# Cross-attention and a mixture of experts in one kernel: the seam between the last heads and the first expert tiles

## The chip, the cores and the metric

One program on one NeuronCore of a Trainium2 chip. The metric is the time of one execution on the device in microseconds (us), here the median of a few runs. The engines are TensorE (PE in the rows, its weight load PEld), VectorE (DVE), ScalarE (ACT), GpSimd (POOL) and SyncE (SP, which only issues transfers).

## The reference, cut to what matters

Sizes: 32 batches of 112 tokens, width 256; 8 heads of 64; 375 context rows beside 112 latents; 8 experts of width 1024, two of them chosen for each token.

```python
x = x + tanh(g_xattn) * xattn(ctx, layernorm(x), mask, ...)      # 8 heads, softmax, @ Wout
h = layernorm(x)
bids = sigmoid(h @ conf_w.T + conf_b) * wealth
top_bids, selected = top_k(bids, 2)
routing = softmax(top_bids)                                      # weights of the two experts
ffn(e) = (silu(h @ gate_w[e].T) * (h @ up_w[e].T)) @ down_w[e].T
x = x + tanh(g_ffn) * sum over the two experts of routing * ffn(e)
```

## The kernel before, in words

All products run on TensorE as three f16 products of a split high and low half (`PARTS`), so most tiles have a "hi" step on ScalarE and a "lo" step on VectorE.

**Attention.** A function `body(b, ...)` on each engine (571 on GpSimd, 766 on ScalarE, 1210 on VectorE, 1550 on TensorE) is written out for batches 0 to 31 and two more turns, 32 and 33, in which only what is left of the last batches runs. A batch has eight slots h, one for each head. In a slot VectorE masks the scores and takes their minimum (`masked_max`, L986), ScalarE takes the exponential (L732), TensorE transposes (L1493), ScalarE and VectorE split the result (`probs_hi` L739, `probs_lo` L992) and TensorE multiplies with the values (oP). The last two heads of a batch are finished in slots 0 to 2 of the next turn. One batch's heads are joined and projected in the next turn too (`heads_out`, `heads_T`, `out_proj`, `residual`), then `rstd1` on GpSimd, `norm2`, `norm2_T`, and one turn later `confidences` and `logits`.

**Routing.** Batches are routed in quads of four. `route` (1049) has 20 steps, small VectorE operations that each wait for the one before: `choose` (0 to 13), `route_rank` (14), `weigh_choice` (15, 16), `place` (17 to 19). `ranks` (1532) counts on TensorE between steps 13 and 14. Then GpSimd scatters the quad's token rows to `routed_rows` in DRAM (`scatter`, L557), two indirect transfers for each batch. The last quad, batches 28 to 31, is routed in two pairs by the table `PAIR_AT`; its rows go out by `scatter_pair`. `QUAD_AT` and `LAST_QUAD_AT` place the steps of the other quads.

**Experts.** Eight experts follow as 63 tiles of 128 routed rows each, in the order of their counts (`order_experts`). `step(t, ...)` runs a tile: `gate_up` (1625) in two halves i of 512 columns, `silu` (L874), `gated` (L1352), `down` (1650) for the tile before, `weigh` (L1365), and an adding scatter into `out` (`add_tile`, L622). The tile's rows come by `load_tile` (564). The first `AHEAD` = 4 tiles have known addresses (`first_i`) and are loaded in turn 32; later ones read theirs from `tile_table` (1396), 18 small VectorE operations which end in `s_tab`. There are `XT_BUFS` = 6 buffers. An expert's weights come as six pieces (`raw`), are squared (`expert_squares`, L826), scaled (`expert_bound`, `expert_pow` L520, `expert_scale`) and split (`expert_hi` L836, `expert_lo` L1204).

**Order.** It is written by hand: each engine executes its own list in order, and semaphores hold an instruction until another engine has counted far enough. Nothing is moved by a scheduler. SyncE's list matters as well: `turn_of` (373) issues a batch's loads and stores, `load_raw` (385) the first two experts' pieces, and between them stand the eight writes of zero rows (`padrows`, L421) behind each expert's rows. In turn 31 of GpSimd's list `rstd1` stands behind four scatters:

```python
                if b == B - 1:
                    scatter(q - 1, 0)
                    scatter(q - 1, 1)
                ...
                if holds(b, 1, B):
                    rstd1(b - 1)
                if b == B - 1:
                    expert_pow(0)
```

## Time and profile before

| what | value |
| --- | --- |
| time, median of 3 runs | 1455.01 us (1454.85 to 1457.35) |
| the profiled execution | 1453.81 us |
| its span, first to last instruction | 1452.2 us |
| busy: PE, PEld, DVE, ACT, POOL | 94%, 67%, 70%, 64%, 33% |
| mean granted TensorE clock | 0.986 of full speed |
| chain that ended last | PE 33%, DMA 3%, all else 1% or less each |
| instructions | 41651 |

The page cuts the span into 40 slices of 36.3 us. TensorE's row reads 9 in nearly all of them, and lower in the first, in slices 23 to 26 and in the last: start, the seam between attention and experts, and end. "Waits" and "idle before" are time in which an engine had nothing to run, with what released it; matmul ends are modelled, so a busy TensorE is not one at its peak.

### The profile page before, as it was taken

The numbers are of one execution on the slowest core, as the hardware profiler recorded it, in microseconds if no ns is written. First come the engines' busy times: TensorE is split into PE (matmuls) and PEld (weight loads), VectorE is DVE, ScalarE is ACT, GpSimd is POOL, SyncE is SP. The second block draws the span as 40 slices with busy tenths as digits, with TensorE's granted clock in tenths as the row PEclk, the third lists the DMA queues.
The fourth block names the chain that finished last, engine by engine and source line by source line (L and its number), as shares of the span: only waits on it lengthen the run. The fifth ranks groups of instructions, "written<-read, shape, count | busy, mean of one in ns | idle before, by whom it ended". The sixth has DMA issues, their size and how long they took to land. (4 is left out here: it accounts for less than half of the span.)

```text
span 1452.2 us, 41651 instructions
## 1 busy us (share of the span) xinstructions
PE 1359.2 (94%) x13880; PEld 972.9 (67%) x13880; DVE 1019.2 (70%) x2553; ACT 933.3 (64%) x1940; POOL 485.9 (33%) x655
## 2 busy tenths in 40 slices
PE   2999999999999999999999958999999999999996
PEld 1466666666666666666666646777877778877784
DVE  4788888888888888888888875665546654334442
ACT  5687877787887878777777765556656553333331
POOL 4323233333433333333432143333344332222221
PEclk9999999999999999999999968999999999999998
DMA  4010101111111101111110335433366743112461
GB/s 117 26 41 26 42 26 43 34 41 46 39 48 32 54 29 41 45 33 53 35 37 14 114 109 157 106 82 94 103 206 175 229 153 91 31 31 34 117 201 16
DMA packets 54866, 107.16 MB, mean 74 GB/s; under 512 B 10832, under 2 KB 32720, under 8 KB 54672
## 3 DMA queue, kind: packets, MB, share of 16 engines
q0 software_dynamic: 23712, 55.71, 14.9%
q1 hardware_dynamic: 30112, 47.75, 10.5%
q8 instruction: 127, 2.08, 0.6%
q10 hardware_dynamic: 848, 1.07, 0.3%
q14 instruction: 67, 0.55, 0.1%
HBM read 69.16 MB, written 35.34 MB: 72 GB/s over the span
## 5 line engine op out<-in xcount | busy, mean ns | idle before, releaser
L874 ACT ACTIVATE sg<-gP,consts 128x512 f32<-128x512 f32 x126 | 86.4, 686 | 240.3 <-PE uP L1435 240.3
L1352 DVE SCALAR_TENSOR_TENSOR act_h<-uP,consts,sg 128x512 f32<-128x512 f32 x126 | 94.6, 750 | 206.8 <-ACT sg L874 202.8
L1435 PE MATMUL fP<-zTs,ws 128*128 128x112 f16 (+1 forms) x1536 | 220.5, 294 | 11.4 <-DVE zT L963 5.6
L1435 PE MATMUL fP<-ws,zTs 128*128 128x512 f16 x768 | 186.8, 379 | 0.5 <-DVE kT L976 0.2
L986 DVE CUSTOM_DVE_ANT_0 ms<-simP,madd,sim_undo 112x488 f32<-112x488 f32 x256 | 183.9, 719 | 3.4 <-remote 0.9
L732 ACT ACTIVATE pr<-ms,nmax 112x488 f32<-112x488 f32 x256 | 179.0, 699 | 4.3 <-DVE nmax L986 1.2
L1435 PEld LDWEIGHTS fP<-zTs,ws 128*128 128x128 f16 x1536 | 109.9, 99 | 102.9 <-issue 34.4
L992 DVE SCALAR_TENSOR_TENSOR pT<-ptP,pT 122x448 f16<-122x448 f32 x256 | 157.5, 615 | 30.3 <-ACT pT L739 29.5
L1435 PE MATMUL yP<-W,aT 128*128 (+1 forms) x1512 | 175.4, 273 | 2.5 <-DVE aT L1358 2.5
L1435 PEld LDWEIGHTS yP<-W,aT 128*128 128x128 f16 x1512 | 147.6, 98 | 33.5 <-issue 3.9
L739 ACT ACTIVATE pT<-ptP 122x448 f16<-122x448 f32 x256 | 137.8, 538 | 42.3 <-PE ptP L1493 39.1
L622 POOL DMA_INDIRECT out<-ysb,xt x63 | 105.3, 1672 | 170.9 <-DVE ysb L1365 162.3
L1435 PE MATMUL oP<-v,pT 122*128 122x64 f16 x3072 | 133.5, 194 | 12.4 <-DVE pT L992 7.4
L1493 PE MATMUL ptP<-ident,pr 112*122 112x112 f32 x1024 | 142.3, 261 | 0.5 <-DVE filled L1097 0.5
L1435 PEld LDWEIGHTS oP<-v,pT 122*128 122x128 f16 x3072 | 120.9, 98 | 24.8 <-DVE pT L992 24.6
L497 POOL TENSOR_TENSOR zTs<-zT,zTs 128x1200 f16<-128x1200 f32 x31 | 76.5, 2469 | 174.3 <-ACT zTs L713 174.3
L1493 PEld LDWEIGHTS ptP<-ident,pr 112*122 112x122 f32 x1024 | 115.0, 140 | 25.2 <-issue 1.2
L1435 PEld LDWEIGHTS fP<-ws,zTs 128*128 128x128 f16 x768 | 68.0, 98 | 82.1 <-issue 14.4
L1483 PE MATMUL simP<-kT,qT 64*128 64x488 f16 x768 | 101.5, 368 | 14.5 <-DVE nmax L986 12.3
L976 DVE SCALAR_TENSOR_TENSOR kT<-fP,kT 128x488 f16<-128x488 f32 x128 | 84.8, 663 | 36.6 <-ACT kT L725 36.6
L725 ACT ACTIVATE kT<-fP 128x488 f16<-128x488 f32 x128 | 73.9, 577 | 52.0 <-PE fP L1435 51.9
L569 POOL DMA_DIRECT2D xt<-routed_rows x63 | 36.0, 574 | 211.0 <-issue 181.3
(220 smaller groups left out, 2557.2 us busy)
## 6 DMA issues: line engine op xcount, KB each, us to landing
raw<-wffn POOLq DMA_DIRECT2D x36, 512.0 KB, 6.3
split_experts<-W POOLq DMA_DIRECT2D x12, 1024.0 KB
W<-split_experts SPq DMA_DIRECT2D x16, 768.0 KB
xc<-ctxt SPq DMA_DIRECT2D x32, 375.0 KB
xt<-routed_rows POOLq DMA_DIRECT2D x63, 129.0 KB, 2.5
raw<-wffn SPq DMA_DIRECT2D x12, 512.0 KB, 8.2
xl<-x SPq DMA_DIRECT2D x32, 112.0 KB
xres<-x SPq DMA_DIRECT2D x32, 112.0 KB, 4.5
```

The lines of the kernel that those rows point to most:

```text
L497: nc.gpsimd.tensor_tensor(zTs[p][:, 1, :, :], zT[:, :, :], zTs[p][:, 0, :, :], ALU.subtract).then_inc(s_zsplit, 1)
L622: pool.indirect_dma_start(out[:, :], bass.IndirectOffsetOnAxis(ap=xt[k][:, D:D + 1].bitcast(I32), axis=0), ysb[t % 2][:, :], None, compute ...
L732: nc.scalar.activation(pr[h % 2][:, :], ms[h % 2][:, :], ACT.Exp, bias=nmax[p][:, h:h + 1], scale=-1.0, accum_out=rsum[p][:, h:h + 1]).the ...
L739: nc.scalar.activation(pT[h % 2][:, 0, :, 0:S], ptP[h % 2][0:KR, :, 0:S], ACT.Copy, scale=P_TOP).then_inc(s_pthi, 1)
L874: nc.scalar.activation(sg[i][:, :], gP[i][:, :], ACT.Silu, scale=constant(place, 0)).then_inc(s_silu, 1)
L976: nc.vector.scalar_tensor_tensor(out=o, in0=i, scalar=1.0 / TOP, in1=hi, op0=ALU.mult, op1=ALU.subtract).then_inc(s_plo, 1)
L986: nc.vector.tensor_tensor_reduce(out=ms[h % 2][:, :], in0=simP[h % 2][0:S, 0:NK], in1=madd[p][:, :], scale=sim_undo[0:S, 0:1], scalar=3.0e ...
L992: nc.vector.scalar_tensor_tensor(out=pT[h % 2][:, 1, :, 0:S], in0=ptP[h % 2][0:KR, :, 0:S], scalar=P_TOP, in1=pT[h % 2][:, 0, :, 0:S], op0 ...
L1352: nc.vector.scalar_tensor_tensor(out=act_h[i][:, :], in0=uP[i][:, :], scalar=constant(place, 2), in1=sg[i][:, :], op0=ALU.mult, op1=ALU.mu ...
L1435: last = nc.tensor.matmul(o, lhs(k, a), rhs(k, c), start=n == 0, stop=n == len(todo) - 1)
L1483: last = nc.tensor.matmul(simP[i][:, 0:NK], qT[p][r, a, h // 2, :], kT[p][r, c, h // 2, :], start=t == 0, stop=t == len(PARTS) - 1)
L1493: last = nc.tensor.transpose(ptP[h % 2][0:KR, c, 0:S], pr[h % 2][:, c * KR:(c + 1) * KR], ident[0:S, 0:S])
```

## The change

The added turns 32 and 33 are gone. After batch 31 each engine has a list `tail()` written out by hand, in which the rest of batch 31 and tile 0 stand side by side, and the tile loop starts at t = 1. In `step` t = 1 to 3 stand the remaining parts of the last batch.

- TensorE: the products of tile 0 (`gate_up(0, ...)`) follow the last head's values; `heads_T(31)`, `out_proj(31)`, `norm2_T(31)` and `confidences(31)` stand between products of tiles 0 and 1, `ranks` of the last quad in step 2.
- Expert 0: its pieces are loaded before turn 32's transfers, squared in batches 29 and 30 (`SPLIT_SQ`) instead of 31, scaled in slots 2 and 3 of batch 31, split in slots 5 to 7 and the tail (`SPLIT_AT`).
- Routing: the last quad is routed as one, in steps 1 and 2 (`close`); its scatters go in GpSimd's steps 2 and 3 (`scatter_last`). The weights of the two experts come from a tanh instead of an exponential and a reciprocal. The copies of its token rows move from ScalarE to GpSimd (`copy_last`).
- The tile table is cut into `tile_counts` (step 2), `tile_places` and `tile_rows` (step 3). `AHEAD` is 5, so tile 5 is the first that is loaded by the table; that load stands in GpSimd's step 3 behind the last scatters. Zero rows behind each expert grow from 3 to 5 tiles (`PADT`).
- Expert 1: squares one to a tile (`SQUARES_1`), scale after `tile_rows` at the end of step 3, split in steps 4 and 5.

```diff
-PADT = -(-(2 * S + P - 1) // P)
+PADT = -(-(4 * S + P - 1) // P)
-AHEAD = 4
+AHEAD = 5
+SQUARES_1 = {0: (0,), 1: (1,), 2: (2, 3, 4), 3: (5,)}
+HI_1 = {4: (0, 1, 2), 0: (3, 4, 5)}
-SPLIT_SQ = {(B - 1, h): (h,) for h in range(PIECES)}
-SPLIT_AT = {(B - 1, 7): (0, 1), (B, 0): (2,), (B, 1): (3,), (B, 2): (4,), (B, 6): (5,)}
+SPLIT_SQ = {(B - 3, 7): (0,), (B - 2, 1): (1,), (B - 2, 2): (2,), (B - 2, 5): (3,), (B - 2, 6): (4,), (B - 2, 7): (5,)}
+SPLIT_AT = {(B - 1, 5): (0,), (B - 1, 6): (1,), (B - 1, 7): (2,)}
...
@@ GpSimd @@
+            def tail():
+
+                pool.wait_ge(s_pv, (B - 1) * H + 6)
+                scatter(QUADS - 2, 2)
+                pool.wait_ge(s_ao, B)
+                scatter(QUADS - 2, 3)
+                copy_last(B - 4)
+                copy_last(B - 3)
+                copy_last(B - 2)
+                rstd1(B - 1)
+                copy_last(B - 1)
...
             def step(t, k):
+                if t == 2:
+                    scatter_last(0)
+                    scatter_last(1)
+                if t == 3:
+                    scatter_last(2)
+                    scatter_last(3)
+                    for i in range(4):
+                        pool.wait_ge(s_scat[i], 32 * QUADS)
+                    pool.wait_ge(s_tab, 1)
+                    for n in range(AHEAD, XT_BUFS):
+                        load_tile(n, n)
...
+                if t == 3:
+                    load_tile(6, 6 % XT_BUFS)
+                if 3 <= t < NT - 4:
                     load_tile(t + 4, (t + 4) % XT_BUFS)
                 p = t // SPAN + 1
                 if p < E and t % SPAN == 3:
                     expert_pow(p)
@@ ScalarE @@
+            def tail():
+
+                probs_hi(B - 1, H - 2)
+                expert_hi(0, 3)
+                tile_hi(0, 0)
+                probs_hi(B - 1, H - 1)
+                norm2_out(B - 2)
+                expert_hi(0, 4)
+                silu(0, 0, 0)
+                heads_out_hi(B - 1)
+                tile_hi(1, 1)
+                act_hi(0, 0, 0)
+                expert_hi(0, 5)
+                silu(0, 1, 0)
+                for c in SQUARES_1[0]:
+                    expert_squares(1, c)
@@ VectorE @@
+                if t == 3:
+                    tile_rows()
+                    expert_scale(p)
...
+            def tail():
+
+                probs_lo(B - 1, H - 2)
+                expert_lo(0, 3)
+                tile_lo(0, 0)
+                probs_lo(B - 1, H - 1)
+                sums_inverse(B - 1, 1)
+                heads_out(B - 1, 1)
+                logits(B - 2, (B - 2) % 4)
+                expert_lo(0, 4)
+                gated(0, 0, 0)
+                heads_out_lo(B - 1)
+                tile_lo(1, 1)
+                act_lo(0, 0, 0)
+                expert_lo(0, 5)
+                gated(0, 1, 0)
+                residual(B - 1, 1)
```

TensorE's list, from the last transposition of batch 31 to the second half of tile 0. oP is the last head's product, tP batch 31's joined heads, projection, second norm and confidences, ptP the ranks, xP and gP, uP tile 0. Before:

```order
L1435 MATMUL oP<-v,pT 128x64 [waits s_ptlo]
L1435 MATMUL oP<-v,pT 128x64 x11
L1537 MATMUL ptP<-both,earlier_h 112x2x8 [waits s_ptlo,s_oh]
L1511 MATMUL tP<-ident,ao 128x112 [waits s_z2c,s_ao]
L1435 MATMUL tP<-ws,aoT 112x256 [waits s_aolo]
L1522 MATMUL tP<-ident,z_3 128x112 [waits s_z2]
L1529 MATMUL tP<-confT,z2T 112x8 [waits s_lg,s_z2c]
L1612 MATMUL xP<-ident,xt 128x128 [waits s_xt0]
L1435 MATMUL gP<-xT,W 128x128 [waits s_xtlo,s_there,s_wlo]
```

Now:

```order
L1712 MATMUL xP<-ident,xt 128x128 [waits s_xt0]
L1610 MATMUL tP<-ident,z_2 128x112 [waits s_z2]
L1523 MATMUL oP<-v,pT 128x64 [waits s_ptlo]
L1617 MATMUL tP<-confT,z2T 112x8 [waits s_lg,s_z2c]
L1523 MATMUL gP<-xT,W 128x128 [waits s_xtlo,s_wlo]
L1599 MATMUL tP<-ident,ao 128x112 [waits s_z2c,s_ao,s_lg]
L1712 MATMUL xP<-ident,xt 128x128 [waits s_xtlo,s_xt1]
L1523 MATMUL tP<-ws,aoT 112x256 [waits s_aolo]
L1523 MATMUL gP<-xT,W 128x128 [waits s_xtlo,s_act,s_there,s_wlo]
L1610 MATMUL tP<-ident,z_3 128x112 [waits s_z2]
```

Five waits of batch 31 stood ahead of tile 0's first product; four of them now stand behind it, and the ranks further back still.

GpSimd's list in its steps 2 and 3, behind the first adding scatter (the stores to routed_rows are the last quad's). Now:

```order
L569 DMA routed_rows<-zrow,slot_i 30336x258 [waits s_padw,s_slots,s_zcopy]
L636 DMA out<-ysb,xt 3712x256 [waits s_add,s_yw]
L579 TENSOR_LOAD t_row_i [waits s_scat3,s_scat2,s_tab,s_scat1,s_scat0]
L581 DMA xt<-routed_rows 128x258
L579 TENSOR_LOAD t_row_i [waits s_add]
L521 TENSOR_TENSOR epow<-ebound,minus_half 128x3 [waits s_ech]
L636 DMA out<-ysb,xt 3712x256 [waits s_yw]
```

Four pairs of stores stand around the second row, two on each side; three loads of tiles (5, 6 and 7) stand between the third row and the power of expert 1.

VectorE's list at the end of step 3. The first t_row is the table's, ebits and the ones behind it are the scale of expert 1, act_h is the first half of tile 4. Now:

```order
L1402 TENSOR_SCALAR ysb<-yP,xt,consts 128x256 [waits s_add,s_down,s_ech]
L1502 TENSOR_REDUCE t_row<-past_jump 1x64 [waits s_tabch]
L1508 TENSOR_SCALAR t_row_i<-t_row 1x64 [waits s_tabch]
L1238 TENSOR_SCALAR ebits<-epow 128x3 [waits s_epow]
L1245 RECIPROCAL consts<-eundo 128x2 [waits s_ech]
L1389 SCALAR_TENSOR_TENSOR act_h<-uP,consts,sg 128x512 [waits s_atlo,s_silu,s_ech]
L1395 TENSOR_TENSOR aT<-aP,aT 128x512 [waits s_athi]
```

Before, the whole table stood ahead of tile 0's first act_h; now its last part stands between tiles 3 and 4, with the scale of expert 1 behind it.

## Rows read from the trace of the kernel before

**Rows 1.** Stretches: length, busy PE, PEld, DVE, ACT, POOL, PEclk, DMA share, GB/s.

```profile
780.00:830.00 50.00, 47.78 (x489) 30.93 (x486) 40.13 (x105) 34.98 (x80) 9.21 (x10) 1.00 0.24 83
845.00:882.00 37.00, 19.07 (x150) 16.13 (x151) 27.85 (x99) 15.72 (x33) 17.52 (x21) 0.54 0.62 189
900.00:1440.00 540.00, 535.94 (x5458) 425.83 (x5455) 275.09 (x467) 252.64 (x420) 170.28 (x173) 1.00 0.42 112
```

**Rows 2.** Chain that ended last, in the seam and tile 2: start, us, what.

```profile
857.65 0.53 DVE pT L992
...
859.58 0.69 DVE ao L1004
...
862.78 2.82 PE tP L1435 x12
...
877.08 2.72 PE gP L1435 x24
...
893.32 1.34 PE gP L1435 x24
...
896.44 0.22 PE xP L1612 x2
...
901.87 1.34 PE gP L1435 x24
```

**Rows 3.** VectorE in order: heads 0 and 7 of batch 31, table, tile 3.

```profile
829.98 0.72 DVE L986 CUSTOM_DVE_ANT_0 ms<-simP,madd,sim_undo 112x488 f32<-112x488 f32 x1
...
849.32 0.73 DVE L986 CUSTOM_DVE_ANT_0 ms<-simP,madd,sim_undo 112x488 f32<-112x488 f32 x1 [0.22 <-DVE ebound L1187]
...
853.37 2.48 DVE L1204 SCALAR_TENSOR_TENSOR W<-raw,escale,W 128x1024 f16<-128x1024 f32 x2 [0.48 <-ACT W L836]
...
868.17 0.41 DVE L1031 TENSOR_SCALAR z<-x,mv,rs 112x256 f32<-112x256 f32 x1 [1.24 <-POOL rs L514]
...
878.78 0.68 DVE L1407 TENSOR_TENSOR past<-turn,tile_end 1x512 f32<-1x512 f32 x1
...
880.80 0.68 DVE L1414 TENSOR_TENSOR past_jump<-past,jump 1x512 f32<-1x512 f32 x1
...
882.78 0.18 DVE L1418 TENSOR_SCALAR t_row_i<-t_row 1x64 int32<-1x64 f32 x1
...
908.76 0.75 DVE L1352 SCALAR_TENSOR_TENSOR act_h<-uP,consts,sg 128x512 f32<-128x512 f32 x1 [0.55 <-ACT sg L874]
```

**Rows 4.** ScalarE in order: a square in batch 31, expert 0's first splits, the table load.

```profile
831.43 1.04 ACT L826 ACTIVATE junk<-raw 128x1024 bf16<-128x1024 f32 x1
...
852.11 2.19 ACT L836 ACTIVATE W<-raw,escale 128x1024 f16<-128x1024 f32 x2 [0.98 <-DVE escale L1193]
...
875.90 1.28 ACT L874 ACT_TABLE_LOAD   x1
```

**Rows 5.** GpSimd in order: last scatter, tile loads, power of expert 1.

```profile
883.06 0.94 POOL L557 DMA_INDIRECT routed_rows<-zrow,slot_i  x1 [0.30 <-issue]
889.69 0.60 POOL L569 DMA_DIRECT2D xt<-routed_rows  x1 [5.70 <-issue]
890.86 0.56 POOL L569 DMA_DIRECT2D xt<-routed_rows  x1 [0.57 <-issue]
...
909.19 0.92 POOL L520 TENSOR_TENSOR epow<-ebound,minus_half 128x3 f32<-128x3 f32 x1
```

**Rows 6.** The page's part 6, tile loads: KB each, us from issue to landing.

```profile
xt<-routed_rows POOLq DMA_DIRECT2D x63, 129.0 KB, 2.5
```

**Rows 7.** The clock in stretches of 2 us, columns as in rows 1.

```profile
846.00:848.00 2.00, 0.56 (x3) 0.56 (x4) 1.32 (x7) 1.06 (x3) 0.75 (x2) 0.81 0.19 58
...
880.00:882.00 2.00, 2.00 (x25) 2.00 (x23) 1.83 (x6) 0.01 (x1) 1.39 (x3) 0.66 1.05 425
```

**Rows 8.** SyncE's issues in the seam: zero rows, then expert 1's pieces.

```profile
862.70 9.28 SPq L421 DMA_DIRECT2D routed_rows<-padrows  x8
873.05 3.86 SPq L390 DMA_DIRECT2D raw<-wffn  x6
```

More of the change, by code:

```diff
@@ L401, in _ @@
                     turn_of(g * 2 + k, k)
-            for b in range(B, B + 2):
-                turn_of(b, b % 2)
             sp.wait_ge(s_order, 1)
@@ L406, in _ @@
             load_raw(0)
-            for b in range(B + 2, B + 4):
+            for b in range(B, B + 4):
                 turn_of(b, b % 2)
@@ L572, in body @@
                 p = g % 2
-                quad = g == 3 and holds(b, 7, B - 1)
                 if holds(b, 0, B - 2):
@@ L577, in body @@
                     rows_lo(b + 2, p)
+                if g == 0 and holds(b, 8, B - 1):
+                    scatter(q - 2, 0)
                 if holds(b, 0, B - 4):
@@ L613, in _ @@
             pad_outside()
-            for b in range(B + 2):
+            for b in range(B):
                 body(b, b % 4, b // 4)
+            tail()
             def add_tile(t, k):
@@ L1391, in step, with close, tile_counts @@
                     weigh(t - 1, (k - 1) % 4, last_place)
-                if 1 <= done < E and j in LO_LATE:
-                    for c in LO_LATE[j]:
-                        expert_lo(done, c)
-            def tile_table():
+                if t == 3:
+                    tile_rows()
+                    expert_scale(p)
+                if 1 <= done < E and j in late:
+                    for c in late[j]:
+                        expert_lo(done, c)
+            def close(first, end):
+                for step in range(first, end):
+                    route(QUADS - 1, slice(0, 4), step)
+            def tail():
[14 more added lines that the diff above has]
+                residual(B - 1, 1)
+            def tile_counts():
                 count_rows()
@@ L1418, in tile_table @@
                 nc.vector.tensor_scalar(t_row_i[:, :], t_row[:, :], float(E * CAP), None, ALU.min).then_inc(s_tab, 1)
[L1420 to L1425 removed]
+            for b in range(B):
+                body(b, b % 4, b // 4)
+            tail()
+            held_now = 0
+            for t in range(1, NT + 1):
+                last_held, held_now = held_now, None if t == NT else place_of(t)
+                step(t, t % 4, held_now, last_held)
         @block.tensor
@@ L1602, in _ @@
                     piece(0, 0, n)
-            for b in range(B + 2):
-                body(b, b % 4, b // 4)
             def tile_T(t, k):
```

277 lines of the change are left out of this document (151 added, 126 removed).

## The prediction

> **What bounds the kernel now.** I read the stretches first. In the attention stage TensorE is busy 47.8 of 50 us, in the expert stage 535.9 of 540 [rows 1]: both belong to TensorE, and work that other engines do there is covered. In the seam between them TensorE is busy 19.1 of 37 us at a granted clock of 0.54 of full speed, half of it in the lower of its two levels, 1.2 instead of 2.4 GHz. So the seam is where something can be gained, and only by starting the tiles' products earlier, since behind them TensorE has no gap to give.
>
> The chain of waits says what stands in the seam. The low half of the last head ends at 858.2 (857.65 + 0.53), the heads are joined at 859.58, the projection takes 2.82 us, and after the norm and 20 small routing steps the first product of tile 0 starts at 877.08; tile 2 starts at 893.32 and tile 3 at 901.87, so an undisturbed tile costs 8.6 us [rows 2]. I call the start of tile t's products S(t). The effect on the end of the kernel is the shift of S(5), because from there on both lists are the same.
>
> **The sum**, against the profiled execution of 1453.81 us (span 1452.2; 1.2 us below the median of 1455.01, to which I add the same difference).
>
> *First product of tile 0.* Before, 18.9 us pass from the last low half to that product. Now only the last head's values and two small confidence products stand there. Joining starts 1.4 us after the low half [rows 2], which holds the values; the confidences fit in the rest, so I take 1.4. Gain 17.5 us. For this four pieces of expert 0 must be split and tile 0 transposed by then; both stand ahead of the last low half in the new lists, so they belong to the next term.
>
> *The slots of batch 31.* Six squares of 1.04 us leave ScalarE's list there [rows 4], 6.2 us. Into slots 3, 5, 6 and 7 of VectorE come the scale (seven small steps) and splits of 1.24 us, half of 2.48 [rows 3], each behind ScalarE's half of 1.1 [rows 4]. The same four splits stood ahead of the last low half before, so none is new; but the scale, moved up to slot 3, lengthens it on VectorE. Bounds: nothing gained, or all 6.2 us. Head 0 to head 7 took 19.3 us before [rows 3], and I find VectorE's own work, with the waits for ScalarE's splits, to fill most of that. I take 1.0 us, near the lower end.
>
> *From S(0) to S(2).* It was 16.2 us, with the slow clock at its start in both cases. Added on TensorE are the projection, 1.4 us at full clock (half of 2.82 [rows 2]), the transposition of the heads, and two or three products as small as a tile's transposition, 0.22 each [rows 2]: together 2.3. Then one wait: from the end of the projection (865.60) to the second norm's z took 2.6 us and z itself 0.41 [rows 2, 3], 3.0 in all, and now the first half of tile 1 covers 2.7 of it (893.32 to 896.44, less 0.44 of transposition). VectorE has also a gated half-tile to do first; I take 0.8 us of wait. Loss 3.1 us, bounds 2.5 and 5.
>
> *Squares in batches 29 and 30.* ScalarE was busy 35.0 of 50 us there, TensorE 47.8 [rows 1]. Six squares of 1.04 put some 6 us more into a list which TensorE waits for at every piece. Bounds 0 (they fall into its gaps) and 4; I take 1.5 us lost, since the gaps are mostly shorter than a square.
>
> *Ranks in step 2.* Eight tiny products, 0.3 us lost. The pieces of routing in steps 1 and 2 lie on VectorE, half idle there (275 of 540 us [rows 1]): nothing.
>
> *Tile 5.* This is the new wait. TensorE transposes tile 5 at S(4) + 3.1 (893.32 to 896.44 [rows 2]). Its load needs the table's end. In step 3 VectorE does the second gated half at S(3) + 6.9 (908.76 against 901.87 [rows 2, 3]), 0.75 long; then `tile_places`, 2.0 us (878.78 to 880.80); bound and weighing, 1.0; `tile_rows`, 2.2 us (880.80 to 882.96 [rows 3]). That is S(3) + 12.8, or S(4) + 4.2. GpSimd then reads a register, 0.57 [rows 5], and the load lands 2.5 us after its issue [rows 6]: S(4) + 7.3, so TensorE waits 4.2 us. Behind that load GpSimd issues two more, 1.17 us apart (889.69 to 890.86), before the power of expert 1, 0.92 [rows 5]; VectorE's scale waits for it and blocks tile 4's first gated half: 4.2 + 3.5 + 0.9, scale 1.3, gated 0.75, low half 0.6 is S(4) + 11.3, where `down(3)` could have started at 10.1. Another 1.2 us. The clock adds to it: in the stretch in which TensorE did 0.56 us of work in 2 it fell to 0.81 and then to half, and it came back only 3.8 us after dense products began [rows 2, 7]. 3.8 us at half speed lose 1.9, of which the wait for `down(3)` hides 1.2. Loss 4.2 + 1.2 + 0.7 = 6.1 us. Bounds: 3.5 if VectorE is ahead of this (`tile_rows` can't start before step 3's last product), 9.6 if the last scatters land late. They leave GpSimd at S(4) + 2.0 (eight at 1.24 apart, 0.94 + 0.30); behind the last one before, the next load was 5.7 us late [rows 5], though with the transfer engines full.
>
> Sum: -17.5 - 1.0 + 3.1 + 1.5 + 0.3 + 6.1 = **-7.5 us**: 1446.3 for an execution like the profiled one, 1447.5 as a median.
>
> Costed at nothing: two more table loads on ScalarE, 1.28 us each [rows 4], in step 1. They delay tile 1's second silu by about 1.1 us, which the 5.2 us of `down(0)` and the first half of tile 2 cover. The Trainium skill, "ScalarE: Activation LUTs", section "What ACT_TABLE_LOAD costs", gives a switch as about 2.66 us, because the engine also drains. No row here shows the drain. By that page the routing's last choice would come late enough for `ranks` to hold TensorE for an estimated 1.5 us, and the sum would be -6.0.
>
> The earlier zero rows cost nothing either, if only transfers wait for them. They are 5 tiles each instead of 3, so what took SyncE 9.3 us to issue takes up to 15.5, and expert 1's pieces follow [rows 8]. They start some 16 us earlier, as soon as batch 30 is through, and expert 1's first square can hold ScalarE for a microsecond or two which its slack covers.
>
> **Rivals.**
>
> *The squares set the pace of batch 31* (chance 0.24). ScalarE's squares stretched every slot, and without them 5 us are gained instead of 1. For it: each is longer than most of ScalarE's gaps. Against it: VectorE takes on the scale. The sum becomes -11.5, 1443.5.
>
> *Gained at S(0), lost in the tail* (0.14). ScalarE and VectorE serve heads, weights and tiles from one list, and one late entry holds all of them. If the last head comes 3 us later, the norm's wait is 3 us instead of 0.8, and squares cost 3, the sum is -7.5 + 4 + 2.2 + 1.5, about 0: 1455.
>
> *GpSimd makes it slower* (0.10). The second norm's `rstd1` now stands behind two pairs of scatters and three copies, each of which waits for a landed scatter; all that goes on while zero rows and expert 1's pieces fill the transfer engines (share 0.62 of the whole seam before [rows 1]). GpSimd would be ready at about 866, and the norm wants it at about 871. The point from which it decides is a landing more than 5 us later than that. If scatters land only behind the zero rows and the pieces, some 12 us later, TensorE waits 7 us at the second norm, the clock adds 1.9, and the late landing at tile 5 another 3.5: -7.5 + 12.4 = +4.9, 1460. For it: the 5.7 us of [rows 5]. Against it: those are 5.7, not 12. The Trainium skill, "DMA: Bandwidth & Descriptors", section "SWDGE vs HWDGE vs iDMA", says that GpSimd's and SyncE's transfers enter different queues of a DMA engine, which takes them in turn; by that a scatter isn't kept behind all zero rows, and this rival goes. No run here shows it yet.
>
> **How the numbers follow.** The forecast has 0.52 and is the likeliest. A measurement of this kernel tells about 0.2%, 2.9 us, from no change. Forecast and first rival are faster (0.76), the second the same (0.14), the third slower (0.10). The terms' bounds taken together give -17.4 and +1.4; the range for 8 in 10 reaches from halfway to the best ends, 1441, to the second rival's 1455.5.
>
> **What would show it.** Right: tile 0's first product within 2 us of the last head's values, and 19 us before the old place; a wait of TensorE for tile 5's rows in step 4 of about 4 us, with GpSimd's load just behind the table's last step; `ebits` waiting for `epow` behind it; the clock low again for about 4 us. Wrong: no wait at tile 5, or one that the scatters end; the second norm's transposition waiting over 2 us; head 7 of batch 31 before 845 or after 851 on its own clock.

## The result, and the profile after

The changed kernel takes 1458.07 us (median of 20 runs, 1454.85 to 1462.77) against 1454.93 for the kernel before (20 runs, 1453.03 to 1457.35): ratio 1.0023, 95% interval 1.0016 to 1.0031. It is slower by 0.23%, where 0.5% faster was forecast. The profiled execution took 1456.04 us, its span 1454.1, at a mean clock of 0.987; span and clock of before were 1452.2 and 0.986.

A call is one sitting on one chip, in which kernels are timed side by side. The calls fall into two kinds, in which the kernel before takes 1453 to 1455 us or 1444 to 1446 us (one chip showed both), and each comparison of times is made within one call. I call them the 1455 calls and the 1445 calls; the profiles of this section and of the one ahead of the prediction are of the first kind.

TensorE in order in the changed kernel: the first products of tiles 0, 2, 3, 4 and 5, i.e. S(0) and S(2) to S(5), with what is between.

```profile
856.86 2.72 PE L1523 MATMUL gP<-xT,W 128*128 128x128 f16 x24
...
870.60 0.41 PE L1610 MATMUL tP<-ident,z 112*128 112x112 f32 x2 [1.01 <-DVE z L1068]
...
877.67 1.50 PE L1523 MATMUL gP<-xT,W 128*128 128x128 f16 x24
...
886.64 1.50 PE L1523 MATMUL gP<-xT,W 128*128 128x128 f16 x24
...
890.42 0.22 PE L1523 MATMUL uP<-xT,W 128*128 128x128 f16 x1 [1.00 <-issue]
890.48 0.29 PE L1747 MATMUL aP<-ident,act_h 128*128 128x128 f32 x1
891.13 0.27 PE L1747 MATMUL aP<-ident,act_h 128*128 128x128 f32 x1 [0.37 <-issue]
...
902.37 0.59 PE L1636 MATMUL bP<-esq,ones 128*128 128x6 f32 x2 [4.89 <-ACT junk L837]
902.82 4.55 PE L1523 MATMUL yP<-W,aT 128*128 128x256 f16 x24
907.21 1.50 PE L1523 MATMUL gP<-xT,W 128*128 128x128 f16 x24
...
913.81 0.69 PE L1712 MATMUL xP<-ident,xt 128*128 128x128 f32 x2 [3.32 <-DMA xt<-routed_rows]
...
920.92 1.50 PE L1523 MATMUL gP<-xT,W 128*128 128x128 f16 x24
```

The first products of tiles 2 to 5 in the kernel before, read in the same way (the chain of [rows 2] has these times 0.16 later):

```profile
893.15 1.50 PE L1435 MATMUL gP<-xT,W 128*128 128x128 f16 x24
...
901.71 1.50 PE L1435 MATMUL gP<-xT,W 128*128 128x128 f16 x24
...
910.40 1.50 PE L1435 MATMUL gP<-xT,W 128*128 128x128 f16 x24
...
918.95 1.50 PE L1435 MATMUL gP<-xT,W 128*128 128x128 f16 x24
```

Tile 0 starts 20.2 us earlier (856.86 for 877.08) and tile 3 still 15.1 (886.64 for 901.71). Tile 4 starts at 907.21, where 910.40 was the time before: 11.9 us are gone inside one tile, which takes 20.6 us instead of 8.7. Tile 5's wait adds 5.2, and S(5) is 920.92 against 918.95: 2.0 us late, as the span is 1.9 longer.

Where the 11.9 us went: ScalarE, then the first and the last of GpSimd's eight stores, then the stretches (columns as in [rows 1]), all of the changed kernel.

```profile
888.24 0.19 ACT L837 ACTIVATION_READ_ACCUMULATOR junk<-raw 128x1 f32 x1
899.14 0.69 ACT L882 ACTIVATE sg<-gP,consts 128x512 f32<-128x512 f32 x1 [10.72 <-remote]
```

```profile
886.11 0.99 POOL L569 DMA_INDIRECT routed_rows<-zrow,slot_i  x1 [3.89 <-DVE slot_i L1175]
...
896.75 0.93 POOL L569 DMA_INDIRECT routed_rows<-zrow,slot_i  x1 [0.30 <-issue]
```

```profile
100.00:780.00 680.00, 661.70 (x6909) 438.32 (x6908) 591.48 (x1634) 541.43 (x1226) 243.14 (x368) 1.00 0.13 39
780.00:830.00 50.00, 47.74 (x492) 30.70 (x491) 39.41 (x101) 38.59 (x89) 9.21 (x10) 1.00 0.27 91
845.00:882.00 37.00, 29.99 (x303) 24.92 (x304) 22.54 (x49) 21.38 (x36) 14.28 (x16) 0.77 0.84 258
884.00:888.00 4.00, 4.00 (x50) 3.71 (x49) 3.58 (x20) 3.60 (x6) 1.59 (x2) 1.00 0.09 25
889.00:899.00 10.00, 6.04 (x27) 2.41 (x24) 0.00 (x0) 0.00 (x0) 6.86 (x7) 0.83 0.38 92
899.00:907.00 8.00, 4.63 (x25) 3.51 (x26) 5.11 (x12) 3.69 (x7) 0.00 (x0) 0.57 0.00 0
```

From 889 to 899 ScalarE and VectorE do nothing at all, and TensorE 27 products, some of them one by one with 0.2 to 1.0 us of "issue" ahead. ScalarE waits 10.72 us for silu(0) of tile 3. Its input was there: the last product of that half is the one at 890.42. The releaser is "remote", i.e. the profile finds none. That product was itself late by 1.0 us, so of the 10.7 us some 2 are a wait for input and 8.5 are not. TensorE's first gap begins 3.3 us behind the first store (889.4 against 886.11), and ScalarE goes on 2.4 us behind the start of the last (899.14 against 896.75). GpSimd alone goes on all the time. The wait of bP for expert 1's last square and the half-clock `down(2)` (4.55 us, clock 0.57) are its wake: that square stands on ScalarE behind the silu.

The lines for tile 5 on VectorE and on GpSimd, SyncE's issues, and the first square of expert 1 and a table load on ScalarE, all of the changed kernel:

```profile
909.87 0.18 DVE L1505 TENSOR_SCALAR t_row_i<-t_row 1x64 int32<-1x64 f32 x1
915.66 0.17 DVE L1238 TENSOR_SCALAR ebits<-epow 128x3 int32<-128x3 int32 x1 [5.61 <-POOL epow L521]
```

```profile
911.42 0.60 POOL L581 DMA_DIRECT2D xt<-routed_rows  x1 [13.73 <-issue]
```

```profile
844.23 13.05 SPq L422 DMA_DIRECT2D routed_rows<-padrows  x8
858.69 8.49 SPq L393 DMA_DIRECT2D raw<-wffn  x6
```

```profile
870.02 1.06 ACT L837 ACTIVATE junk<-raw 128x1024 bf16<-128x1024 f32 x1 [3.91 <-DMA raw<-wffn]
...
874.58 0.23 ACT L779 ACTIVATE ex<-lg 112x32 f32<-112x32 f32 x1
874.83 1.28 ACT L882 ACT_TABLE_LOAD   x1
876.12 0.69 ACT L882 ACTIVATE sg<-gP,consts 128x512 f32<-128x512 f32 x1
```

### The profile page after: what moved, and what is told of

Read it like the earlier page. It is cut to its first block, busy times and chain, and to the rows that moved or that the text cites. A ratio compares the mean times of both kernels' runs of the same rounds, so it can differ in the third digit from the quotient of the medians.

```text
span 1454.1 us, 41488 instructions
## 1 busy us (share of the span) xinstructions
PE 1362.5 (94%) x13880; PEld 972.1 (67%) x13880; DVE 1015.2 (70%) x2528; ACT 931.2 (64%) x1932; POOL 487.5 (34%) x659
## 3 DMA queue, kind: packets, MB, share of 16 engines
q0 software_dynamic: 23712, 55.71, 15.1%
q10 hardware_dynamic: 848, 1.07, 0.3%
## 4 chain that ended last, share of the span: by engine, by line
PE 70%; DVE 9%; ACT 6%; issue 6%; DMA 5%; SPq 1%; POOL 1%; another core or an unknown queue 1%; POOLq 0%; DVEq 0%; ACTq 0%
PE fP L1523 19%; PE yP L1523 10%; PE uP L1523 10%; PE gP L1523 9%; PE simP L1571 5%; PE ptP L1581 4%; PE tP L1523 3%; PE oP L1523 3%; DVE ms L1023 2%; DVE pT L1029 2%; DMA out<-ysb,xt 2%; DMA raw<-wffn 2%; PE aP L1747 2%; DVE ao L1041 1%; ACT z L715 1%
## 5 line engine op out<-in xcount | busy, mean ns | idle before, releaser
L1523 PE MATMUL oP<-v,pT 122*128 122x64 f16 x3072 | 133.5, 194 | 17.4 <-DVE pT L1029 12.6
L1523 PE MATMUL uP<-xT,W 128*128 128x128 f16 x1512 | 106.1, 220 | 1.0 <-issue 1.0
```

The source lines that it names most:

```text
L1523: last = nc.tensor.matmul(o, lhs(k, a), rhs(k, c), start=n == 0, stop=n == len(todo) - 1)
```

## The experiments

S(t) and the span are from one profiled execution of each kernel, in us; the ratio to the kernel before is from all the executions of both in the same call, and not from the medians alone:

| kernel | call | S(0) | S(2) | S(3) | S(4) | S(5) | span | ratio (95%) |
| --- | --- | --- | --- | --- | --- | --- | --- | --- |
| before, first profile | 1455 | 877.08 | 893.15 | 901.71 | 910.40 | 918.95 | 1452.2 | |
| before, e9 | 1455 | 878.25 | 894.80 | 903.35 | 912.04 | 920.59 | 1452.6 | |
| before, e15 | 1445 | 872.32 | 889.21 | 897.76 | 906.45 | 915.00 | 1444.0 | |
| changed, first profile | 1455 | 856.86 | 877.67 | 886.64 | 907.21 | 920.92 | 1454.1 | 1.0023 (1.0016 to 1.0031) |
| changed, e1 | 1455 | 857.38 | 883.45 | 892.42 | 912.49 | 926.20 | 1460.7 | 1.0045 (1.0032 to 1.0058) |
| changed, e10 | 1455 | 857.40 | 880.74 | 889.71 | 910.91 | 924.84 | 1458.0 | 1.0027 (1.0014 to 1.0040) |
| changed, e14 | 1445 | 857.00 | 884.51 | 893.48 | 902.46 | 918.94 | 1453.0 | 1.0024 (1.0014 to 1.0033) |
| no last stores, e2 | 1455 | 857.84 | 882.48 | 891.45 | 900.42 | 914.71 | 1446.7 | 0.9963 (0.9952 to 0.9974) |
| spaced, e3 | 1455 | 857.48 | 884.20 | 893.17 | 902.14 | 919.19 | 1450.9 | 0.9985 (0.9976 to 0.9995) |
| squares later, e11 | 1455 | 856.96 | 876.09 | 885.06 | 905.25 | 920.33 | 1451.7 | 1.0007 (0.9997 to 1.0016) |
| squares later, e7 | 1445 | 856.87 | 876.29 | 885.26 | 894.23 | 910.86 | 1442.0 | 0.9977 (0.9968 to 0.9987) |
| spaced, pieces first, e8 | 1445 | 856.74 | 875.59 | 884.56 | 893.53 | 910.12 | 1438.5 | 0.9972 (0.9962 to 0.9983) |
| the same, e16 | 1445 | 856.84 | 876.65 | 885.62 | 894.59 | 911.61 | 1441.9 | 0.9975 (0.9966 to 0.9984) |
| tile 5 later, e12 | 1455 | 857.33 | 876.97 | 885.94 | 906.44 | 916.29 | 1450.7 | 0.9991 (0.9981 to 1.0002) |
| all together, e13 | 1445 | 856.49 | 876.68 | 885.65 | 894.62 | 908.69 | 1440.1 | 0.9966 (0.9952 to 0.9979) |
| e13, power first, e17 | 1445 | 856.90 | 876.79 | 885.76 | 894.73 | 905.82 | 1435.3 | 0.9959 (0.9946 to 0.9971) |
| the same, e18 | 1455 | 857.06 | 877.28 | 886.25 | 895.22 | 908.92 | 1442.3 | 0.9942 (0.9925 to 0.9958) |

Behind S(5) the lists are the same, but the profiles of this table still need 528.4 to 534.5 us from there to the end. So the span of one execution says less about an edit than the ratio does.

**Is the stall the kernel's, and is it the stores?** e1 is the changed kernel again.

> The changed kernel once more, nothing edited. In its first profile ScalarE's silu of tile 3 stood 10.7 us (888.4 to 899.1) with its inputs there, TensorE went product by product with gaps and VectorE stood too, and S(4) came 20.6 us behind S(3) where 8.7 is normal: 11.9 us lost. If that stall belongs to the kernel, it is there again at the same silu, 8 to 13 us long, and the time is 1458 again. If it is a chance of the one execution, the profile has no idle time of ScalarE over 3 us in tile 3, S(4) is about 895, and the profiled time is about 1444, or the runs spread between 1444 and 1460.

It is there again (silu(0) of tile 3, 9.30 us, S(4) - S(3) = 20.1), 1461.98 us. A second loss shows: ScalarE's first square of expert 1 waited 6.77 us and TensorE 3.19 us for the confidences of batch 31.

```diff
             def step(t, k):
-                if t == 2:
-                    scatter_last(0)
...
-                        pool.wait_ge(s_scat[i], 32 * QUADS)
                 if t == 3:
                     pool.wait_ge(s_tab, 1)
```

> The eight stores of the last quad's rows on GpSimd (four pairs, in tiles 2 and 3) are left out, so the last quad's tokens get no expert output. Theory A: the unbroken series of eight indirect stores on GpSimd, 886 to 898, holds up the other engines. Then the stall is gone, S(4) - S(3) is about 8.8 us instead of 20.6, the wait for tile 5's rows stays (3 to 4 us), and the time is 11 to 13 us less, about 1446. Rival B: the stall sits at a place in ScalarE's or TensorE's instruction list and has nothing to do with the stores: it stays, and the time is 1457 to 1458. Rival C: it belongs to expert 1's squares or the routing's tanh in the same tiles: also unchanged.

1448.33 us, 13.6 less than e1 in the same call. S(4) - S(3) is 8.97, and no wait without a releaser is left. B and C fall: the lists of TensorE, ScalarE and VectorE are unchanged. What went with the stores is GpSimd's wait for their landing.

```diff
                 if t == 2:
                     scatter_last(0)
-                    scatter_last(1)
                 if t == 3:
+                    pool.wait_ge(s_gu, 7)
+                    scatter_last(1)
+                    pool.wait_ge(s_gu, 8)
                     scatter_last(2)
+                    pool.wait_ge(s_act, 8)
                     scatter_last(3)
```

> The same eight stores, but no longer in one row: the first pair in tile 2, the second behind the first half of tile 3, the third behind its second half, the fourth behind its second gated half. Theory A (a long unbroken series is what stalls): the stall shrinks to under 2 us, S(4) - S(3) about 9 to 10.5 us, time 1446 to 1448. Theory A' (each store costs the other engines its share, whatever the spacing): about 10 us are still lost, in four pieces of 2 to 3 us, time about 1457. Rival B: unchanged, one stall of 10 us at the silu of tile 3.

1452.73 us, 9.3 less than e1, and S(4) - S(3) is 8.97. The spacing was poor (a gap of 1.0 us behind the first pair and of 0.3 behind an adding scatter, then six stores in a row), and yet the long stall is gone. What is left of it is short: VectorE waits 1.7 us at 896.8 and again at 905.0, and from the start of the sixth store of the row, 904.02, TensorE's products go one by one (2.37 us of work from 903 to 907), now in step 4:

```profile
903.48 0.50 PE L1526 MATMUL uP<-xT,W 128*128 128x128 f16 x6
904.21 0.22 PE L1526 MATMUL uP<-xT,W 128*128 128x128 f16 x1 [0.23 <-issue]
904.95 0.33 PE L1526 MATMUL uP<-xT,W 128*128 128x128 f16 x3 [0.52 <-issue]
```

So neither "each store costs its share" (10 us) nor a plain count of stores in a row fits. In order, GpSimd had four stores, the adding scatter and four stores without a gap; now it has two, the gap of 1.0 us, the adding scatter and six. Whether the gap or the earlier adding scatter avoids the long stall was not told apart.

```diff
+            for _ in range(100):
+                apart(act)
             for b in range(B):
```

(and the same for TensorE)

> 100 semaphore increments that nobody waits for are put ahead of batch 0 in ScalarE's and in TensorE's list, so that every later instruction lies 100 places further on in the instruction store; the order of the work and the stores are as in the changed kernel. They cost up to about 3 us at the start. Theory A: the stall stays at the silu of tile 3, 8 to 13 us, time 1458 to 1461. Rival B (a fetch of instructions that falls due just there): the stall is gone or sits at another instruction, and the time is 1446 to 1450.

The stall stays at the same silu, 10.69 us, S(4) - S(3) = 20.4: B falls. The time was 1476.98, because the increments, priced at 3 us, cost 14.6 (S(0) 871.98), some 0.15 us each. TensorE stands 14.06 us ahead of its product at 62.06, in batch 0.

**Does any row of eight do it?** e5 is the kernel before with its stores bunched, e6 the changed kernel with plain stores. Both fell into a 1445 call.

```diff
-                if quad and b < B - 1:
-                    scatter(q - 1, 0)
-                if g < 3 and holds(b, 8, B - 1):
-                    scatter(q - 2, g + 1)
+                if g == 0 and holds(b, 8, B - 1):
+                    for i in range(4):
+                        scatter(q - 2, i)
```

> The kernel before, with one edit in the attention stage: the four pairs of indirect stores of each quad 0 to 5, which GpSimd issues one pair a batch some 24 us apart, are issued as one row of eight in batches 8, 12, ... 28. Its trace had no idle time without a releaser there. Theory A (a long unbroken series of indirect stores on GpSimd holds up the other engines): six stalls of TensorE, ScalarE or VectorE appear, each 2 to 10 us long and each beginning 2 to 4 us behind the first store of a series; the time is 12 to 60 us more. If the stall belongs to the seam alone (its code or its other transfers), the time is that of the kernel before within 3 us.

1496.56 us, but with no "remote" wait in the whole trace. The edit made a wait of its own: ScalarE's copy of the next quad's rows stood 6.11 us for the landing of the row (271.86), and TensorE 6.15 behind it. The 51 us tell nothing of theory A.

```diff
                 for c in range(2):
-                    pool.indirect_dma_start(xs[:, :], bass.IndirectOffsetOnAxis(ap=slot_i[:, c, g:g + 1], axis=0),
-                                            zrow[:, g, c, :], None).then_inc(s_scat[g], 16)
+                    pool.dma_start(scr[g * 2 + c, :, :], zrow[:, g, c, :]).then_inc(s_scat[g], 16)
```

> The changed kernel with the eight indirect stores of the last quad replaced by eight plain ones of the same rows, by GpSimd too, to a scratch tensor (so the last quad's tokens get no expert output). Theory A1 (it is the indirect form): no stall in tile 3, S(4) - S(3) about 9 us, time as without the stores, 1448. Theory A2 (any eight transfers of these rows in a row by GpSimd): the stall of about 10 us is there, time about 1458.

1446.50 us, ratio 1.0006 (0.9996 to 1.0016), S(4) - S(3) = 8.97. I first read this as "the indirect form is the cause". That reading fell with e7 and e14, which have no stall in a 1445 call with their indirect stores in place. Whether plain stores would stall in a 1455 call was not tried.

**The late piece.** e7 moves expert 1's first square; e11 is the same kernel in a 1455 call.

```diff
-SQUARES_1 = {0: (0,), 1: (1,), 2: (2, 3, 4), 3: (5,)}
+SQUARES_1 = {0: (), 1: (0, 1), 2: (2, 3, 4), 3: (5,)}
```

> The changed kernel with the first square of expert 1 moved on ScalarE from ahead of silu(0) of tile 1 to the end of tile 1's step. In the two profiles of the changed kernel that square waited 3.9 and 6.8 us for expert 1's first piece, behind 13 to 13.7 us of zero rows on SyncE; in the second TensorE's confidences of batch 31 waited 3.2 us for it and S(2) - S(1) was 17.0 us instead of 10.9. If that is the second loss: that wait is gone, S(2) - S(1) is about 11, the stall of tile 3 stays, and the median is 1452 to 1455, with the runs closer together. If ScalarE had slack, the time is that of the changed kernel, 1458 to 1462.

> The kernel with expert 1's first square later, once more, beside the changed kernel on one chip. It ran on the faster chip only, without a stall in tile 3, though its row of stores is unbroken. If the chip of this call takes 1455 for the kernel before: theory D expects the stall of 9 to 11 us and S(2) - S(1) of about 10.5. If it takes 1445: 0.995 to 0.998 of before and 5 to 7 us less than the changed kernel, all from S(2).

S(2) is 876.29 and 876.09, against 877.67 to 884.51 in the four profiles of the changed kernel; e11 takes 1456.02 beside e10's 1459.71, 3.7 less. So the square's wait is the second loss, and its size follows the landing of the piece: it waited 3.91, 5.77, 6.77 and 8.25 us in the first profile, e10, e1 and e14, and S(2) is 1.5, 4.5, 7.3 and 8.3 us behind 876.2. TensorE waits for the `z2T` that stands behind the square in ScalarE's list, 0.38, 2.19, 3.19 and 4.67 us. In e14, the square and the products of batch 31's confidences:

```profile
874.08 1.06 ACT L837 ACTIVATE junk<-raw 128x1024 bf16<-128x1024 f32 x1 [8.25 <-DMA raw<-wffn]
```

```profile
876.10 0.91 PE L1617 MATMUL tP<-confT,z2T 128*112 128x8 f32 x4 [4.67 <-ACT z2T L767]
```

The clock adds to it: in e14 it is 1.00 up to 873, while TensorE does only 0.9 us of work from 873 to 877, and 0.50 from 877 to 881, where in the first profile it stays at 1.00. The spread of the changed kernel's runs over 8 us fits that. And e7 had no stall in tile 3, e11 10.66 us of it: the same kernel, so whether the stall is there goes with the kind of call.

```diff
                              padrows[:, :].unsqueeze(1).to_broadcast([P, PADT, XW])).then_inc(s_padw, 16)
+                if e in (2, 4, 6):
+                    load_raw(1, {2: (0,), 4: (1,), 6: (2,)}[e])
-            load_raw(1)
+            load_raw(1, (3, 4, 5))
```

> The spaced stores, and on SyncE the first three pieces of expert 1 issued between the zero rows (behind experts 2, 4 and 6) instead of behind all of them. If both losses are as read: ScalarE's first square of expert 1 waits less than 1 us, S(2) - S(1) is about 11 us, and the time is 5 to 6 us less than with the spaced stores alone (1452.7), so about 1447. If the pieces come no earlier, because the transfer engines and not SyncE are the limit, it stays at 1452 to 1453.

0.9972 (0.9962 to 0.9983), and 0.9975 (0.9966 to 0.9984) again as e16. The square waits for nothing, S(2) - S(1) is 10.35: the pieces come in time once SyncE's list lets them, though the transfer engines' share from 845 to 882 is 0.84 in the changed kernel and 0.90 here. That is another cure for the same loss, not an addition to it. Both fell into 1445 calls, where there was no stall to avoid, so the forecast of 1447, made for a 1455 call, was not tested.

**The two kinds of call.**

> The kernel before, unedited, for a profile from the chip of this call: the calls so far fell on two chips, which ran it in 1454.8 and 1445.4 us. If the chips differ by stalls like that of tile 3, a profile at 1445 has none of the small ones that the first profile had (ScalarE 1.8 us and VectorE 0.9 us without a local releaser at 846, beside four stores of GpSimd in a row), and one at 1455 has them again.

> The changed kernel on the chip of this call. Theory D (the stall needs the row of stores and a chip on which something else disturbs): where the kernel before takes 1455, the stall of 9 to 11 us in tile 3 is there and the ratio is 1.002 to 1.005; where it takes 1445, the stall is gone, S(4) - S(3) is about 9 us, and the ratio is about 1.000. Theory A (the row of stores alone): S(4) - S(3) is about 20 us on either.

> The changed kernel on the chip of this call, beside the next. On a chip with 1455 for before: the stall again (ScalarE stands from 2.3 us behind the first store to 2.4 us behind the start of the last), ratio 1.002 to 1.005. On one with 1445: no stall, S(4) - S(3) 9 us, ratio 0.998 to 1.003, which with 1.002 to 1.005 would say that the kernel before loses as much there in another place.

> The kernel before for a profile on this chip. Only on a chip that runs it in 1445 is there something to tell: then the stretch in which it is 9 us shorter than in the first profile (attention, seam or tiles) shows what the kernel before pays for on the other chips.

e9 has the waits without a releaser (VectorE 2.4, ScalarE 1.9 us beside a row of four stores), e15 none. The 1445 call of e15 fell on the chip that gave 1455 in e1 to e4, so the chip, as these expectations had it, is not what divides the calls. e14 has no stall, S(4) - S(3) = 8.97, and is still slower, 1.0024. The last expectation then asked where the kernel before is faster. The stretch 100:780 of e15 and, in the second fence, of the kernel before in its first profile, columns as in [rows 1]:

```profile
100.00:780.00 680.00, 661.65 (x6909) 438.24 (x6908) 591.36 (x1633) 541.48 (x1227) 242.94 (x368) 1.00 0.14 39
```

```profile
100.00:780.00 680.00, 658.18 (x6853) 435.10 (x6852) 587.63 (x1618) 537.52 (x1216) 243.49 (x368) 1.00 0.14 39
```

TensorE gets 3.5 us less done there in the 1455 call. ScalarE's first work behind a pair of stores (the stores start at 246.16 and 247.55 in e9, at 246.06 and 247.46 in e15), e9 first and then e15:

```profile
249.24 1.22 ACT L707 ACTIVATE zT<-fP,lnv 128x375 f32<-128x375 f32 x2 [1.06 <-PE fP L1452]
```

```profile
248.11 1.22 ACT L707 ACTIVATE zT<-fP,lnv 128x375 f32<-128x375 f32 x2
```

The transposition that it needs ended at 248.11 in e9 and at 248.01 in e15, so ScalarE went on 1.1 us late in the one and 0.1 in the other. By the next pair e9 is 1.0 us behind e15 (268.32 for 267.30). The quad's other three pairs add nothing (318.27 for 317.24 at the fourth), and each further quad adds 0.5 to 0.8 at its first pair alone: 4.9 us by the pair at 775.94, and 5.9 by S(0). The changed kernel has that first pair 8 us later in the batch (254.34), and no such loss: its stretch 100:780 is 661.70 even in the 1455 call, and its pair of stores near 797 starts at 797.44 in e10 and 797.41 in e14. So in a 1455 call both kernels seem to pay for their stores, one in the attention stage in small pieces, the other in one piece in tile 3. For the kernel before this is read from where the time goes; it was not run without those pairs. And it is not the whole difference between e9 and e15, 8.6 us of span: 5.6 are there by S(5), and 3.0 come behind it, whose cause is open. The ratios of the two kinds agree (1.0027, 1.0024) by different ledgers.

**Tile 5.** e12 adds to e11 the pieces of e8, the power earlier, and:

```diff
                 down(t - 1, 1 - q, last_byte)
+                if t == 4:
+                    tile_T(t + 1, (t + 1) % XT_BUFS)
```

> The same, and also: expert 1's first three pieces issued between the zero rows, its power on GpSimd ahead of the wait for the table, and in step 4 the transposition and split of tile 5 behind down(3) instead of ahead of the second half. S(5) - S(4) was 13.7 to 16.6 us where 8.6 is undisturbed: 3.3 to 5.8 us of wait for tile 5's rows and 2 to 3 us of products at the lower clock behind it. If that wait is the cost: S(5) - S(4) is 9.5 to 11 us, and the time is 5 to 7 us less than with expert 1's squares later alone. If the rows come later still, or ScalarE's list holds the next splits, it gains under 2 us.

S(5) - S(4) is 9.85 us, but only 2.5 us of time are gained beside e11 (1453.49 for 1456.02). In this kernel the stall of tile 3 had let the stores finish before step 4. And 1.3 us have only moved on: the next tile, behind the shifted transposition, takes 9.85 instead of 8.55 (9.7 in e17 and e18). e13 spaces the stores as well:

> Everything that gained, together: spaced stores, expert 1's first square later and its first three pieces between the zero rows, power and tile 5's transposition later. On a chip that takes 1455 for the kernel before, the spaced stores gave 8.7 us back (e3 against e1), the square 4 to 5 and tile 5 another 2.5: forecast 0.991 to 0.995 of before, 1442 to 1447. If spacing loses its worth where the stores now end later against the table, 0.996 to 0.999. On a chip that takes 1445, without the stall: 0.993 to 0.997.

> The kernel of e8 (spaced stores, pieces between the zero rows, tile 5 as in the changed kernel), beside e13, so that tile 5's part is told apart: 2 to 3 us more than e13. On a chip that takes 1455 for before: 0.994 to 0.997 of it.

e13: 0.9966 (0.9952 to 0.9979), 1.4 us less than e16. S(5) - S(4) is 14.1: `down(3)` waited 2.73 us, and the reason is GpSimd's power, which I had put behind the landing of the stores. e17 puts it ahead:

```diff
+                    expert_pow(1)
                     for i in range(4):
                         pool.wait_ge(s_scat[i], 32 * QUADS)
-                    expert_pow(1)
```

> As e13, with the power of expert 1 one place earlier on GpSimd: behind the last store, but ahead of the wait for the stores' landing (in e13 it started 2.0 us behind that wait, at 899.7, VectorE's scale waited for it until 900.6, and down(3) waited 2.7 us for tile 4's split). Expected: ebits at about 898.4, no wait of down(3) over 1 us, S(5) - S(4) 10 to 11 us instead of 14, and 3 to 4 us less than e13 in proportion to before: 0.993 to 0.995 in a call that runs the kernel before in 1445. In a call with 1455, where e13 was not run: 0.990 to 0.995. If tile 5's rows, and not the scale, end the step: under 1 us gained, 0.996.

> The kernel of e17 in another call. Nothing new is tried; it is to tell whether the gain also holds in a call that runs the kernel before in 1455, in which the unbroken row of stores stood ScalarE still for 10.7 us: there 0.990 to 0.996 if the spaced stores avoid the stall here too, 0.997 to 1.001 if it is back (12.5 us between S(3) and S(4) more than 8.7, or in pieces). In a call with 1445: 0.996 again.

Step 4 of e17 on TensorE:

```profile
894.73 1.50 PE L1533 MATMUL gP<-xT,W 128*128 128x128 f16 x24
...
901.36 2.79 PE L1533 MATMUL yP<-W,aT 128*128 128x256 f16 x24 [0.76 <-DVE aT L1403]
904.25 0.44 PE L1722 MATMUL xP<-ident,xt 128*128 128x128 f32 x2
905.82 2.03 PE L1533 MATMUL gP<-xT,W 128*128 128x128 f16 x24 [1.13 <-DVE xT L1387]
```

S(5) - S(4) is 11.1, and 1438.72 us against 1444.40: 0.9959, a little above what was expected. That interval overlaps the one of e13, so what the one line gained is shown by the trace (`down(3)` waits 0.76 us for 2.73) and not by the times. In the 1455 call of e18 it is 1444.23 against 1452.94, 0.9942, with S(4) - S(3) = 8.97: this kernel beats the one before in both kinds of call. S(5) - S(4) is 13.7 for the 11.1 of e17. The stall is down to three gaps of TensorE, 1.7 us in all, at the end of its row of six, and 0.95 us of VectorE:

```profile
897.24 0.55 DVE L1410 TENSOR_SCALAR ysb<-yP,xt,consts 128x256 f32<-128x256 f32 x1 [0.95 <-issue]
```

## Why the prediction was wrong, point by point

Forecast and measured, in us, by the profiles (the first two in a 1455 call, e14 against e15 in a 1445 call):

| stretch | forecast | 1455 | 1445 |
| --- | --- | --- | --- |
| up to S(0) | -17.0 | -20.2 | -15.3 |
| S(0) to S(2) | +3.1 | +4.7 | +10.6 |
| S(2) to S(4) | +0.3 | +12.3 | +0.7 |
| S(4) to S(5) | +6.1 | +5.2 | +7.9 |
| sum to S(5) | -7.5 | +2.0 | +3.9 |
| behind S(5) | 0 | -0.1 | +5.1 |

Two things that the prediction costed at nothing made -7.5 into +3.1: the eight stores as they act on engines that don't wait for them (11.9 us in tile 3, in 1455 calls), and expert 1's first square (1.5 to 8.3 us at S(2), in both kinds). With neither, in e7, the gain is 3.2 us of 1445.35 and still not 7.5; there batch 31 and tile 5 were taken too cheap.

**First product of tile 0 (-17.5): right.** It starts 1.4 us behind the start of the last head's values (855.48 to 856.86), as taken; in the 1445 pair (e14 against e15) the step is -17.2.

**Batch 31 and the squares (-1.0 and +1.5): wrong.** The last values start at 855.62 in e14 against 853.71 in e15, +1.9 for the +0.5 forecast. The squares in batches 29 and 30 cost 0.3 us (head 0 of batch 31 at 825.81 for 825.47). Batch 31 became 1.6 us longer instead of 1.0 shorter: from head 0 to head 7 it takes 22.4 us instead of 19.3, and one slot 6.15 (838.25 to 844.40), in which VectorE waits 1.71 us for ScalarE's half of the first split. The splits are not new, but they stood behind head 7 before. In the 1455 calls it looks like a gain of 2.8 us (855.48 against 858.24). That is the kernel before paying for its pairs. I took its attention stage as undisturbed, since its waits name proper releasers, and one trace alone can't show that 0.7 to 0.9 us in each quad are abnormal.

**S(0) to S(2) (+3.1): right in its own terms, wrong by what I costed at nothing.** With the square out of the way it is +2.6 (e11 against e9: 19.13 for 16.55) and +2.5 (e7 against e15). The second norm's wait was 1.01 us for 0.8. The step that failed is "expert 1's first square can hold ScalarE for a microsecond or two which its slack covers". I had the 15.5 us of zero rows on SyncE (13.05 to 13.8 measured) but never followed the square to what stands behind it in ScalarE's list: silu(0) of tile 1 and `norm2_out(31)`, for which TensorE waits. Worth 1.5 to 8.3 us of S(2) by the landing, 3.7 in the medians of e10 and e11, and some 6.8 between the ratios of e14 and e7 (1.0024, 0.9977).

**S(2) to S(4): +0.3 forecast, +12.3 measured in a 1455 call, +0.7 in a 1445 call.** Nothing in the forecast stood for it. I had asked of the eight stores only what waits for them, and not what they do to engines that don't. The trace had a warning, ScalarE's and VectorE's waits without a local releaser at 846 (1.76 and 0.94 us), beside four stores in a row. I had passed them by as too small, and in that profile they cost nothing in the end: the last values come 17.0 us behind the first of the four stores there as in e15.

**Tile 5 (+6.1, bounds 3.5 and 9.6): right in the 1455 call, the end of the wait wrong in the other.** Measured +5.2, and +7.9 in e14. The chain is the one described: 3.32 us of wait, `ebits` waiting 5.61 for `epow`, the clock at 0.55 from 914 to 917. Here the table ends the wait (909.87, then the load at 911.42). Without the stall the stores' landing does, which the prediction had named as a sign of being wrong: in e14 the table is ready at 906.0, GpSimd's last store ends at 905.4, the load goes at 908.58, and TensorE waits 5.32 us (in e13 the table is ready at 898.3 and GpSimd waits for the stores until 899.68).

**Table loads (nothing): right.** 1.28 us each, and ScalarE goes on with no gap (874.83 + 1.28, then 876.12). The drain that the Trainium skill gives in "ScalarE: Activation LUTs", "What ACT_TABLE_LOAD costs", would make 2.66; the trace does not show it.

**The rivals.** The first fell: without its squares batch 31 is longer. The second names what the square did, one late entry of ScalarE's list that holds all the others, but its late entry was the last head. The third has the right sign, for GpSimd's stores did make it slower, but by another mechanism: the second norm waited 1.0 us and no more. The Trainium skill, "SBUF — State Buffer", section "Who interferes with whom", states that TensorE and ScalarE wait on nobody and that DMA never contends with a compute engine. As a rule on the memory's ports that may stand. As a promise that a transfer issued by GpSimd costs the others nothing it doesn't hold here: ScalarE stood 10.7 us, 8.5 of them with its input there.

**The sum in the 1445 call**, e14 against e15: -15.3 to S(0), +10.6 to S(2), +0.7 to S(4), +7.9 to S(5), together +3.9; forecast to S(5), -7.5. This profile is of an execution of 1454.94 with the latest piece; the median of e14 is 1448.74, +3.2 on the kernel before. Its span is 9.0 us longer than that of e15, and not 3.9: 5.1 are lost behind S(5), some 3 of them in the last three tiles, where TensorE waits 2.93 us for an expert's weights (`W<-split_experts`, 1416.97). The forecast took that part as equal.

**Small slips in the sum.** S(2) to S(5) were read from the chain, 0.16 later than the first products, so S(0) to S(2) was 16.1 before and not 16.2. The range's lower end, 1441, counts half the way to -17.4 from the profiled execution; from the median it is 1442.6. Neither changes the outcome.

**What stays open:** what differs between the two kinds of call; what holds up the engines during the row (that signals between engines arrive late would fit ScalarE's silu and the 1.06 us in the attention stage, but not the gaps inside a product, and was only argued); and why the four stores from 868.45 to 873.55 in the kernel before cost nothing visible. The packets of the traces rule out two simple answers. The row's own transfers run alike with and without the stall: the first packet 1.6 us behind the first store, the last 12.8 (first profile) and 13.7 us (e14) behind it, 0.13 us for one in the mean in both. And the engines did not stand for 10 us because a load of instructions came late: in each profile one of 16 KB falls into the row, 1.06 to 1.67 us long in the first, e1, e10, e11 and e12, 0.95 and 1.07 in e14 and e7; in the first it starts at 890.08, when ScalarE already stands.

## What to carry to other kernels

Indirect stores of GpSimd have a price beyond their own engine: in a row of eight they stopped the others for about as long as the row lasted, in some calls. Space them or put them where nobody has work, and take a wait without a releaser beside such stores, however short, as a warning of what a longer row may cost. When transfers are moved ahead of others in a queue, follow the delayed one to its consumer and then to everything behind that consumer in its engine's list. And measure in more than one call: here the unbroken row brought a stall of some 11 us in every 1455 call and in no 1445 call, and the ratio hid it, because the kernel before lost time of its own.

## What the runs showed of the hardware

- The row of eight stores (0.94 us each, 0.30 apart, with an adding scatter between) kept ScalarE idle for 9.3 to 10.7 us in all six profiles of 1455 calls that have it unbroken (the first, e1, e4, e10, e11, e12); in five of them ScalarE went on 2.3 to 2.4 us behind the start of the last store. In the two 1445 profiles with the same row (e7, e14) there was no such idle time, and two of the eight stores took 1.34 to 1.36 us.
- Of a quad's four pairs of stores in the kernel before, the first cost 0.5 to 0.9 us in a 1455 call against a 1445 call, the other three nothing (e9 against e15).
- 100 semaphore increments by themselves in each of TensorE's and ScalarE's lists made S(0) 14.6 us later, about 0.15 us for one (e4 against e1).
- A table load of ScalarE took 1.28 us with 0.02 us or less of gap on either side (874.58 + 0.23, 874.83 + 1.28, 876.12).
